# An attention kernel on one core: the seam between blocks a head later, one-time loads in small pieces, signs spread over five heads

## The reference

```
q  = (xn @ Wq_c.T + bq_c) @ Wq_up.T + bq_up        # 32 heads of 128 + 64
kv = xn @ Wkv_c.T + bkv_c                          # 64 latents + 64 rope
attn = softmax(q @ k.T / sqrt(192))                # per head, 1024 x 1024
o_h  = attn @ v_h                                  # 128 wide
out  = einsum('bhsv,Hv->bsH', o, Wo) + bo          # sum over the heads
x = x + out
x = x + ffn(layernorm(x))                          # three 512 x 512 layers of signs, s0, s1, s2
```

## Time and profile before

| | us |
|---|---|
| median of the runs (1705.19 to 1707.86) | 1705.82 |
| the profiled execution | 1698.23 |
| its span, first to last instruction | 1696.4 |
| PE busy | 1617.4 (95%) |
| DVE busy | 1522.8 (90%) |
| ACT busy | 1371.2 (81%) |
| GpSimd busy | 942.5 (56%) |
| q1, the hardware DMA queue (transposes and loads) | 94.8% of 16 engines' span |

### The profile page before, as it was taken

One profiled execution on the slowest core, in us unless ns is written; L12 is line 12 of the kernel. 1 busy time (PEld: TensorE's weight loads), 2 busy tenths in 40 slices (PEclk: granted clock), 3 DMA queues, 4 the chain that ended last, 5 costly groups with the idle time before them and its releaser, 6 DMA issues. The chain is left out here.

```text
span 1696.4 us, 24098 instructions
## 1 busy us (share of the span) xinstructions
PE 1617.4 (95%) x7572; PEld 758.7 (45%) x7572; DVE 1522.8 (90%) x2080; ACT 1371.2 (81%) x1979; POOL 942.5 (56%) x1610
## 2 busy tenths in 40 slices
PE   7979899999999999999999999999999999999899
PEld 6734344444444444444444444444444444444344
DVE  5569898999998999999989999999989999999765
ACT  5668788888887889888979888988879888898422
POOL 3346555666655666666646655665545665564320
PEclk9989999999999999999999999999999999999999
DMA  6469999999999999999989999999999999999611
GB/s 218 155 115 211 203 199 205 206 201 187 201 195 166 201 202 200 200 198 196 202 160 203 196 199 198 199 200 198 196 165 196 204 198 199 194 194 201 145 50 50
DMA packets 1090457, 314.10 MB, mean 185 GB/s; under 512 B 1068352, under 2 KB 1078880, under 8 KB 1090336
## 3 DMA queue, kind: packets, MB, share of 16 engines
q1 hardware_dynamic: 1084288, 296.09, 94.8%
q0 software_dynamic: 6048, 16.52, 4.2%
HBM read 35.71 MB, written 8.39 MB: 26 GB/s over the span
## 5 line engine op out<-in xcount | busy, mean ns | idle before, releaser
L952 ACT ACTIVATE S<-S,shift,unscale 128x1024 f32<-128x1024 f32 x512 | 606.2, 1184 | 145.6 <-DVE shift L1007 144.3
L1000 DVE TENSOR_REDUCE mx<-S 128x1 f32<-128x1024 f32 x512 | 623.2, 1217 | 49.7 <-PE S L851 35.2
L992 DVE TENSOR_TENSOR halves<-S,halves 128x1024 f16<-128x1024 f32 x512 | 623.2, 1217 | 27.7 <-ACT halves L961 15.0
L961 ACT ACTIVATE halves<-S 128x1024 f16<-128x1024 f32 x512 | 526.1, 1027 | 26.0 <-DMA PT<-halves 14.2
L849 PE MATMUL S<-kvTH,qeH 128*128 128x512 f16 x1024 | 396.7, 387 | 19.7 <-DVE halves L992 17.9
L850 PE MATMUL S<-kvTL,qeH 128*128 128x512 f16 x1024 | 391.3, 382 | 0.0
L851 PE MATMUL S<-kvTH,qeL 128*128 128x512 f16 x1024 | 391.0, 382 | 0.0
L787 POOL CAST onormH<-onorm 128x512 fp32r<-128x512 f32 x127 | 77.6, 611 | 488.4 <-DVE onorm L1047 488.4
L862 PE MATMUL O<-PT,kvn 128*128 128x512 f16 x1024 | 241.9, 379 | 0.0
L849 PEld LDWEIGHTS S<-kvTH,qeH 128*128 128x128 f16 x1024 | 99.5, 97 | 255.9 <-DVE halves L992 145.3
L789 POOL TENSOR_TENSOR onormL<-onorm,onormH 64x512 fp32r<-64x512 f32 x127 | 163.6, 1288 | 10.2
(11 more groups left out here) (263 smaller groups left out, 1989.4 us busy)
## 6 DMA issues: line engine op xcount, KB each, us to landing
weff_whole<-weff_scratch POOLq DMA_DIRECT2D x126, 128.0 KB, 4.6
PT<-halves SPq DMA_TRANSPOSE x512, 4.9
raw<-in_raw SPq DMA_DIRECT2D x8, 772.0 KB, 5.9
weff_scratch<-w_split SPq DMA_DIRECT2D x8, 512.0 KB, 6.3
x<-in_x SPq DMA_DIRECT2D x4, 1024.0 KB, 8.3
x_all<-in_x SPq DMA_DIRECT2D x3, 1024.0 KB, 6.4
out<-y SPq DMA_DIRECT2D x3, 1024.0 KB, 4.3
wv<-in_wv SPq DMA_DIRECT2D x4, 512.0 KB, 5.1
```

What stands on the lines that cost most here:

```text
L952: nc.scalar.activation(S[:, t % SLOTS, :], S[:, t % SLOTS, :], ACT.Exp, bias=shift[:, col:col + 1], scale=keep["unscale"][:, 0:1], accum_o ...
L961: nc.scalar.activation(halves[u][:, 0, :], S[:, t % SLOTS, :], ACT.Copy).then_inc(high_out, 1)
L992: v.tensor_tensor(halves[u][:, 1, :], S[:, t % SLOTS, :], halves[u][:, 0, :], ALU.subtract).then_inc(low_out, 1)
L1000: v.reduce_max(mx[:, col:col + 1], S[:, t % SLOTS, :], AX.X, negate=True).then_inc(max_ready, 1)
```

## The change

- The loads: `wv` comes in eight pieces of 256 KB instead of four of 512 KB, behind the odd steps 1 to 13 (the first ahead of step 0). x0 comes in four pieces of 256 KB behind steps 15, 17, 19 and 21, `wo` behind 16, `bo` behind 18, the three layers behind 23, 25 and 27. `ffn_in` counts to 12 loads now instead of 9. GpSimd's table `ahead` moves accordingly: `biased` to steps 30 to 33, `signed_rows` to 38, the weights to 42 and on.
- The seam: at h = 2 `project_tile` goes behind the query projection, and there is no output at that step. `bv` and the output of head 0 of the block go into h = 3, behind `scores(1)`. `output` has the head and the `stop` flag as arguments now. On DVE `add_projection` goes from u = 3 of h = 2 to u = 0 of h = 3, and the statistics from h = 3 to h = 4.
- The signs: one of the five instructions at each of the steps 29 to 33.

```diff
-WP = 4
+FFN_LOADS = 12
+WP = 8
...
-                    if g in (1, 3, 5):
-                        load_values((g + 1) // 2)
-                    if g == 7:
-                        sp.dma_start(keep["x0"][:], dram["x"][0:BLK, :].rearrange("(t p) d -> p t d", p=P)).then_inc(ffn_in, 16)
-                    if g == 9:
+                    if g % 2 and g // 2 + 1 < WP:
+                        load_values(g // 2 + 1)
+                    if g in (15, 17, 19, 21):
+                        t = (g - 15) // 2
+                        sp.dma_start(keep["x0"][:, t, :], dram["x"][t * P:(t + 1) * P, :]).then_inc(ffn_in, 16)
+                    if g == 16:
                         sp.dma_start(keep["wo"][:], dram["woT"]).then_inc(ffn_in, 16)
-                    if g == 11:
+                    if g == 18:
                         sp.dma_start(keep["bo"][:], dram["bo"].partition_broadcast(P)).then_inc(ffn_in, 16)
-                    if g in (13, 14, 15):
-                        load_layer(g - 13)
+                    if g in (23, 25, 27):
+                        load_layer((g - 23) // 2)
...
-            ahead = {20 + t: partial(biased, t) for t in range(UN)} | {28: rows, 36: signed_rows}
-            ahead |= {40 + 2 * (KT * j + k): partial(weights, j, k) for j in range(3) for k in range(KT)}
+            ahead = {30 + t: partial(biased, t) for t in range(UN)} | {28: rows, 38: signed_rows}
+            ahead |= {42 + 2 * (KT * j + k): partial(weights, j, k) for j in range(3) for k in range(KT)}
...
-                def output():
-                    pe.wait_ge(wv_split, g - 1)
-                    pe.wait_ge(onorm_high, g - 1)
-                    pe.wait_ge(onorm_low, g - 1)
...
+                def output(k, last):
+                    pe.wait_ge(wv_split, k + 1)
+                    pe.wait_ge(onorm_high, k + 1)
+                    pe.wait_ge(onorm_low, k + 1)
...
                 if on:
                     scores(1)
+                    if h == 3 and b:
+                        pe.wait_ge(summed0, b)
+                        mm(V[:], bv[:], ones[:], start=True, stop=False)
+                        output(g - 3, False)
...
-                        if (u, h) == (3, 2) and b:
+                        if (u, h) == (0, 3) and b:
                             add_projection(b - 1)
-                        if (u, h) == (3, 3) and b:
+                        if (u, h) == (3, 4) and b:
                             statistics(b - 1)
-                        if u == 3 and g == 24:
-                            signs()
+                        if u == 3 and 29 <= g < 34:
+                            signs(g - 29)
```

More of the change, by code:

```diff
@@ L806, in body @@
                 if g in ahead:
-                    pool.wait_ge(ffn_in, 16 * 9)
+                    pool.wait_ge(ffn_in, 16 * FFN_LOADS)
                     ahead[g]()
@@ L867, in values @@
                     last.then_inc(pv_done, 1)
-                def output():
-                    pe.wait_ge(wv_split, g - 1)
-                    pe.wait_ge(onorm_high, g - 1)
-                    pe.wait_ge(onorm_low, g - 1)
-                    mm(V[:], wvH[par][:], onormH[:], start=False, stop=False)
-                    mm(V[:], wvH[par][0:KVL, :], onormL[:], start=False, stop=False)
-                    mm(V[:], wvL[par][:], onormH[0:KVL, :], start=False, stop=h == (1 if on else 0)).then_inc(wv_done, 1)
+                def output(k, last):
+                    pe.wait_ge(wv_split, k + 1)
+                    pe.wait_ge(onorm_high, k + 1)
+                    pe.wait_ge(onorm_low, k + 1)
+                    mm(V[:], wvH[k % 2][:], onormH[:], start=False, stop=False)
+                    mm(V[:], wvH[k % 2][0:KVL, :], onormL[:], start=False, stop=False)
+                    mm(V[:], wvL[k % 2][:], onormH[0:KVL, :], start=False, stop=last).then_inc(wv_done, 1)
                 def project_tile(t):
@@ L910, in body @@
                     scores(3)
[L911 to L914, removed]
                     if exists(g + 2):
@@ L920, in body @@
                         project_queries(g + 2)
[L921 to L926, removed]
+                    if h == 2 and b:
+                        pe.wait_ge(vsum_out, b)
+                        pe.wait_ge(ffn_in, 16 * FFN_LOADS)
+                        project_tile(b - 1)
+                    if h == 2 and not b:
+                        pe.wait_ge(bv_in, 16)
+                        pe.wait_ge(ones_set, 1)
                         mm(V[:], bv[:], ones[:], start=True, stop=False)
-                if exists(g - 2) and exists(g - 1):
-                    output()
+                if exists(g - 2) and exists(g - 1) and not (h == 2 and b and on):
+                    output(g - 2, h == (1 if on else 0))
             steps(pe, body)
@@ L1017, in statistics, with signs @@
                     v.bn_stats(keep["st0"][:, t, :], keep["x0"][:, t, :]).then_inc(stats0, 1)
-                def signs():
+                def signs(step):
                     sign, sc, factor = keep["sign"], keep["sc"], keep["factor"]
[L1023 to L1033, removed]
+                    if step == 0:
+                        dve.wait_ge(ffn_in, 16 * FFN_LOADS)
+                        v.tensor_scalar(sign[:], sc[:, 0:2], 0.0, 2.0, ALU.is_ge, ALU.mult).then_inc(sign_ready, 1)
+                    if step == 1:
+                        dve.wait_ge(sign_ready, 1)
+                        v.tensor_scalar(sign[:], sign[:], -1.0, None, ALU.add).then_inc(sign_ready, 1)
+                    if step == 2:
+                        dve.wait_ge(sign_ready, 2)
+                        v.tensor_tensor(sized[:], sc[:, 0:2], sign[:], ALU.mult).then_inc(sign_ready, 1)
+                    if step == 3:
+                        dve.wait_ge(sign_ready, 3)
+                        v.scalar_tensor_tensor(out=factor[:], in0=sized[:, 0:1], scalar=1024.0, in1=sized[:, 1:2], op0=ALU.mult,
+                                               op1=ALU.mult).then_inc(sign_ready, 1)
+                    if step == 4:
+                        dve.wait_ge(sign_ready, 4)
+                        v.tensor_tensor(factor[:], factor[:], sc[:, 2:3], ALU.mult)
                 def reciprocals():
```

## The result

| | before | changed |
|---|---|---|
| median of 8 runs, us | 1705.82 (1701.13 to 1709.58) | 1693.45 (1688.07 to 1699.5) |
| ratio, 95% interval | | 0.9929 (0.9908 to 0.995) |
| the profiled execution | 1698.23 | 1691.86 |
| its span | 1696.4 | 1689.8 |
| granted clock, mean | 0.989 | 0.996 |

The change is faster by 0.7%, 12 us (8.5 to 15.7). The forecast was 21.5 us, 1684.3; the measured time is inside its range (1677 to 1695), near the upper end.

What follows compares the result with a forecast made beforehand. VectorE and TensorE were taken to have no room in attention, with long steps at seams and loads. Gains of 13.3 (seam), 1.1 (signs) and 7.1 (loads) sum to 21.5 us, from 1705.8 to 1684.3 us, range 1677 to 1695.

Steps and rivals of the forecast that it cites:

- The seam: At the three seams: 3.1 us each in place of 6.46, 8.06 and 8.06, so 13.3 us gained.
- The add at 7.84: At h = 3, DVE's add of the projected tile starts 7.84 us behind the reciprocal of h = 2.
- The choice of 2.15 us for bias and output: At the seam, `bv` and three output matmuls take 2.15 us on PE, as in head 2 of block 0.
- The signs: Heads 29 to 33: five instructions, one a head, partly hidden, 1.1 of 2.2 us gained.
- The loads: One-time loads in attention, spread in 256 KB pieces: 5.9 us less transpose waiting plus 1.2 us, 7.1 us gained.
- each head gives back d: On SP's queue in attention, each head makes up d = 0.6 us of the transposes' delay.
- p = 1.9: On SP's queue, each 256 KB piece loaded in attention delays the transposes by p = 1.9 us.
- as forecast: Seam and loads as computed, each within some us: 1680 to 1689 us; chance 0.60.
- The loads vanish: In attention no transpose is late any more, 6.7 us more gained, 1677.6 us; chance 0.16.
- small pieces are dear: Cutting x0 and wv into smaller loads costs 13 us, 1697.6 us; chance 0.06.
- slower: Every piece makes the transpose behind it on SP's queue late, 17.6 us lost, 1709.0 us; chance 0.05.
- The clock falls at the new seam too: PE's clock drops at the new seams, 3.5 us a seam, 1694.8 us; chance 0.13.

Runs made afterwards that it cites:

- e1: The kernel before with only the seam of the change, loads and signs as before: 1693.94 us against 1703.23, ratio 0.9939.
- e3: The kernel before with only the signs spread, one instruction in each of steps 29 to 33: 1704.12 us against 1703.23, ratio 0.9993.
- e5: The changed kernel without the loads behind steps 15 to 27, output not the reference's: 1685.92 us, ratio 0.9885.
- e6: The kernel of e4 with loads spread wider, wv pieces behind every third step and x0 behind 28 to 48: 1688.6 us, ratio 0.9892.
- e9: The kernel of e4 with wo, bo, flags and scales loaded in prepare, x0 pieces behind steps 15, 18, 21, 24: 1682.75 us, ratio 0.9868.
- e10: The changed kernel with only the three scale loads moved into prepare: 1687.99 us, ratio 0.9908.
- the two sets: The changed kernel timed twice against the kernel before: 1693.45 us, ratio 0.9929, then six runs (e8) at 1686.22 us, ratio 0.990.
- e8: The changed kernel once more, unaltered, for a second profile: 1686.22 us, ratio 0.990.
- e4: The changed kernel with bias and a block's first output one place later, between scores 2 and 3 of h = 3: 1684.32 us, ratio 0.988.
- e7: The kernel of e4 with loads, bias adds and GpSimd weights as before the change: 1689.28 us, ratio 0.9882.

## Why the prediction was right or wrong

**The seam: right, and in its steps.** 13.3 us forecast, 13.2 in e1, 12.9 by the means of all seams. The add at 7.84, values at 10.72 and `max` 2 3.1 us late are the numbers of the sum. PE's wait was 0.57 instead of 0.7. The choice of 2.15 us for bias and output, from a row of block 0, was what made it fit.

**The signs: the mechanism right, a size wrong.** 1.1 us forecast, 2.2 in the trace of e3. The step that failed gave the third instruction 0.88 and the fifth 0.93 us, their lengths in the chain. Apart they take 0.35 and 0.32, and they hide altogether. Why they were long in the chain is not shown: the second and the fourth also needed the one before and took 0.17 and 0.16 there.

**The loads: wrong.** 7.1 us forecast, nothing measured: the mean surplus is 13.9 us with the old loads and 14.4 with the new. The step that failed is "each head gives back d", with d = 0.6 and p = 1.9. It came from five single waits (0, 1.89, 0.21; 1.12, 1.48), and single waits scatter by about a microsecond from trace to trace. The new order has 28 heads in the sum where the old had 15, and these thirteen give back 7.8 us in the model; one more piece takes 1.9 of them. e5 shows that heads without loads give back next to nothing while the transposes are late, and e6 that a third head between pieces does not help either. What counts is how much is loaded inside attention, not where: e5 and e9 are the only ones that lower the sum by more than the scatter. From e5 and e10 a piece costs 0.5 us and a scale load about 1, if e10 is taken at its word; if not, a piece costs up to 0.9. One part of the term came true, the least: the longest wait, behind the 1 MB load, is gone (5.2 us before, none over 2.0 now). The forecast did not say that the granted clock would gain by it: it is 0.97 or 0.98 in steps 1 to 16 of all four traces with the old loads, 0.99 or 1.00 in those without. Neither shows in the sums above.

What a head gives back can be read from SP's own rows, and this the forecast did not look at. The issues of transposes in steps 17 to 33, of the kernel before, the changed one and e5 (duration in ns, shortest/median/longest):

```profile
L678 SPq DMA_TRANSPOSE PT<-halves x69: 1382/2419/4387, 309.1 to 501.6; - x69
```
```profile
L679 SPq DMA_TRANSPOSE PT<-halves x70: 1583/2816/3999, 297.9 to 500.1; - x70
```
```profile
L682 SPq DMA_TRANSPOSE PT<-halves x69: 1842/2723/4165, 305.3 to 498.4; - x69
```

The four issues of a step, in the mean of steps 17 to 32, hold SP for 10.2 us before, 11.1 in the changed kernel, and 11.1 in e5, which has no load there. Of a step of 11.25 us that leaves 1.0 us to catch up in the first, and 0.2 in the other two. So d was not a constant: 0.6 lies between what a head gives back when the transposes are in time and what it gives back when they are late.

With the two corrected terms the sum is 13.2 + 2.2 + 0 = 15.4 us. The measured 12 (8.5 to 15.7) and 17 (12 to 22) in the two sets stand around that.

That the first of them fell into the range of 1677 to 1695 is partly luck. The upper end was set for a clock that falls at all three seams, not for loads that gain nothing. The case "as forecast" (1680 to 1689) was missed by 4 us in the first set and hit in the second, in both with a term of 7 us that did not exist.

**The rivals.** "The loads vanish", "small pieces are dear" and "slower" did not happen: the largest single wait of ACT went from 5.2 to 2.0 us and the sum stayed. As to the rule cited from the Trainium skill (DMA: Bandwidth & Descriptors, section Bandwidth), the surplus with pieces of 256 KB is the same as with 512 and 1024 KB within the scatter, so no run here shows a loss by cutting. The landing times do agree with the rule: a piece of `wv` lands 3.6 us behind its issue with 256 KB and 5.1 with 512. The first time, 1693.45, is nearest to that of "The clock falls at the new seam too" (1694.8), but it came about otherwise: this case happened at one seam of that trace only. Of the fifteen seams of the changed form in five traces (changed, e1, e5, e8, e10) three had a granted clock of 0.94 over two steps and 1.6 us more. The granted clock was 0.50 there for some 3.4 us. That is 0.3 us a seam in the mean, and 1.6 rather than 3.5 where it happens. The twelve seams of e4's form (e4, e6, e7, e9), where PE does not wait in the middle of h = 3, all kept 1.00.

**What stays open.** In the old order the transposes catch up within a few heads behind the last load (surplus -0.1 and 0.1 in steps 17 to 33 of e3 and e7). In the new order, with no load for nearly eighteen heads (e5), they don't: from the end of `low` to the landing of its transpose it takes 7.5 us in the mean of steps 17 to 32 of e5, 8.2 in the changed kernel and 5.6 before. The rows of SP say how they stay late, by issues that take 11.1 us of a step. Why an issue takes longer once they are late is not shown; GpSimd's weight loads on the other queue are a candidate that wasn't tried.

## What to carry to other kernels

Where PE waits for another engine, ask what is queued behind that wait, and move the waiting instruction to a place at which its data is nearly or already there. That was worth most of this gain (13 us of 15 by the traces), and it could be computed in advance from one undisturbed step. Here, spreading transfers over a queue that had almost no room moved the waits and kept their sum; taking five pieces and the scales out of the stage lowered it. A rate worked out from a handful of single waits is not a rate: look at the busy time of the queue's own engine over a whole stretch, and at a second trace, before a term rests on it.

## What the runs showed of the hardware

- Five small DVE instructions, each needing the one before, took 0.35, 0.17, 0.85, 0.16 and 1.00 us in a row (the two of kind `TENSOR_TENSOR` were the long ones), and 0.32 to 0.38 us each a head apart.
- The issue of a load of 0.5 KB, broadcast to 128 partitions, held SP for 0.54 us, that of 256 KB for 0.58 and that of 1 MB for 0.73. Three of the small ones cost about 1 us of waiting each in one trace (e10).
- With late transposes SP's four transpose issues took 11.1 us of a step of 11.25, with or without loads between them (changed kernel and e5); with transposes in time 10.2.
- In 3 of 15 new seams, with the same instructions, the granted clock went to 0.50 for some 3.4 us. It fell 11.2 us behind the reciprocal of h = 2, 2.6 us after the end of a PE wait of 0.57 us; in the changed kernel PE was busy 10.63 of the 12.01 us of that step. In the other 12 it stayed at 1.00.
